# A third layer's activation queue: the first half of the exponentials ahead of the norm, the copy of the transposed norms behind the second half

## The reference

```
x = x + self_attention(norm(x))                # causal, queries = keys = values = norm(x)
x = x + cross_attention(norm(x), ctx, bias)    # a bias of 16 x 128 x 128 for each sequence
h = norm(x)
z = norm1(h) ; o = softmax(q k^T / sqrt(8)) v  # q, k, v = z @ wq + bq, z @ wk + bk, z @ wv + bv
y = h + (o @ wo + bo)
hn2 = norm2(y)
expert = argmax(hn2 @ gate_w + gate_b)         # one of 8
x = x + y + relu(hn2 @ w1[expert] + b1) @ w2[expert] + b2
```

## Time and profile before

| what | value |
|---|---|
| median of three runs | 399.95 us (399.87 to 401.6) |
| the profiled execution | 401.7 us, of which its span 400.0 us |
| mean granted TensorE clock | 0.935 |
| PE busy | 307.4 us (77% of the span) |
| DVE busy | 263.2 us (66%) |
| POOL busy | 253.2 us (63%) |
| ACT busy | 195.0 us (49%) |
| third layer | some 205 to 320 us of the span |

### The profile page before, as it was taken

One profiled execution on the slowest core, in us unless ns is written; L12 is line 12 of the kernel. 1 busy time (PEld: TensorE's weight loads), 2 busy tenths in 40 slices (PEclk: granted clock), 3 DMA queues, 4 the chain that ended last, 5 costly groups with the idle time before them and its releaser, 6 DMA issues.

```text
span 400.0 us, 10159 instructions
## 1 busy us (share of the span) xinstructions
PE 307.4 (77%) x3458; PEld 204.3 (51%) x3458; DVE 263.2 (66%) x670; ACT 195.0 (49%) x387; POOL 253.2 (63%) x361
## 2 busy tenths in 40 slices
PE   0578868767888999999688887778887751399993
PEld 0134434324766666666464444444444441399993
DVE  5137783487899899998365545476676466177873
ACT  3258775533546455655335536544545610145551
POOL 5873653346699889899996665586743554025544
PEclk9989998997899999999999989999999975599998
DMA  6109999500477887832113998433000111244110
GB/s 172 13 2 261 341 337 338 152 13 2 134 197 182 195 213 159 215 46 26 15 15 48 282 340 256 168 137 124 28 27 1 53 46 43 86 134 142 44 30 4
DMA packets 69186, 50.19 MB, mean 125 GB/s; under 512 B 36093, under 2 KB 50816, under 8 KB 69136
## 3 DMA queue, kind: packets, MB, share of 16 engines
q1 hardware_dynamic: 54960, 21.18, 22.4%
q10 hardware_dynamic: 12672, 25.20, 20.2%
q0 software_dynamic: 1504, 3.16, 2.3%
HBM read 28.48 MB, written 21.50 MB: 125 GB/s over the span
## 4 chain that ended last, share of the span: by engine, by line
PE 46%; DVE 18%; issue 14%; POOL 10%; ACT 8%; DMA 1%; SPq 0%; ACTq 0%; POOLq 0%; DVEq 0%
PE pair_banks L626 26%; PE work_bank L626 8%; DVE biased L1172 5%; PE pair_banks L629 5%; ACT xn L957 4%; DVE pair_banks L1194 3%; PE small_bank L629 3%; PE work_bank L629 3%; POOL biased L452 2%; DVE rowmax L1187 2%; DVE att L1219 2%; PE small_bank L626 1%; DVE rowsum_inv L1213 1%; POOL rstd L406 1%; ACT outT L1003 1%
## 5 line engine op out<-in xcount | busy, mean ns | idle before, releaser
L997 ACT ACTIVATE probs<-pair_banks 128x1024 f32<-128x1024 f32 x96 | 98.0, 1024 | 61.3 <-PE pair_banks L629 36.8
L452 POOL TENSOR_TENSOR biased<-biased,rowmax 128x1024 f32<-128x1024 f32 x32 | 60.5, 1897 | 16.5 <-DVE rowmax L1179 16.3
L626 PE MATMUL work_bank<-probs,vaug 128*32 128x128 f32 x1536 | 54.2, 284 | 2.7 <-DVE vaug L1157 1.2
L626 PEld LDWEIGHTS work_bank<-probs,vaug 128*32 128x32 f32 x1536 | 40.8, 113 | 17.7 <-issue 8.1
L1187 DVE TENSOR_REDUCE rowmax<-pair_banks 128x8 f32<-128x1024 f32 x32 | 38.9, 1217 | 14.0 <-PE pair_banks L626 13.9
L1172 DVE TENSOR_TENSOR biased<-pair_banks,bias_in 128x1024 f32<-128x1024 f32 x32 | 38.8, 1214 | 8.6 <-PE pair_banks L626 5.1
L519 POOL DMA_INDIRECT out<-biased x23 | 22.5, 978 | 33.4 <-DVE biased L1324 32.7
L626 PE MATMUL pair_banks<-k_lane,qT 32*128 32x512 f32 x256 | 38.6, 673 | 3.8 <-DVE biased L1172 2.4
L626 PE MATMUL pair_banks<-q_lane,kT 32*128 32x512 f32 x256 | 38.8, 678 | 1.8 <-DVE biased L1172 1.7
L629 PEld LDWEIGHTS pair_banks<-ident,biased 128*128 128x128 f32 x256 | 29.7, 149 | 18.7 <-issue 13.6
L1179 DVE TENSOR_REDUCE rowmax<-biased 128x8 f32<-128x1024 f32 x32 | 38.9, 1214 | 0.5
(11 more groups left out here) (190 smaller groups left out, 563.0 us busy)
## 6 DMA issues: line engine op xcount, KB each, us to landing
routed_rows<-cleared SPq DMA_DIRECT2D x8, 1028.0 KB, 15.2
routed_rows<-cleared ACTq DMA_DIRECT2D x8, 1028.0 KB, 6.7
bias_in<-in_w SPq DMA_DIRECT2D x16, 256.0 KB, 8.0
biased<-routed_rows SPq DMA_DIRECT2D x23, 128.5 KB, 2.1
ctx_in<-in_ctx SPq DMA_DIRECT2D x8, 128.0 KB, 6.1
att_scratch<-att SPq DMA_DIRECT2D x16, 64.0 KB, 5.4
att_rows<-att_scratch SPq DMA_DIRECT2D x16, 64.0 KB, 4.5
x_sb<-in_x SPq DMA_DIRECT2D x1, 640.0 KB, 5.4
```

Of the source, the lines that this page charges most:

```text
L452: nc.gpsimd.tensor_tensor(v, v, rowmax[:, b % 2, 8 * half:8 * half + 8].unsqueeze(2).to_broadcast([128, 8, S]), ALU.subtract).then_inc(s_s ...
L626: return nc.tensor.matmul(o, lhsT, rhs, start=start, stop=stop, **kw)
L997: nc.scalar.activation(probs[:, b % 2, 2 * half:2 * half + 2, :], pair("exp", b, half), ACT.Exp, scale=1.0 if layer(b) == CROSS else SCALE ...
```

## The change

In ACT's loop the calls of a slot change places, in the third layer alone. The first half of the exponentials runs directly behind `take_attT`, ahead of `normalise` and `last_normalise`. `take_hT` of the third layer and the early `take_hn2T` (slots 43, 45 and 47) run behind the second half of the exponentials. `take_qk` keeps its place between the two halves, the first two layers keep their order, and no other engine's code changes.

```
                 if c is not None:
                     take_attT(c)
+                if FIRST_FFN <= b < NB:
+                    exponentials(b, 0)
                 if FIRST_FFN <= b and b % 2 == 0 and q + 3 < NP:
                     normalise(q + 3)
                 if b in NORMS:
                     last_normalise(NORMS[b])
-                if FIRST_FFN <= b < NB:
-                    exponentials(b, 0)
                 if b % 2 == 1 and CROSS_PAIR <= q + 3 < NP:
                     take_qk(q + 3)
-                if b % 2 == 0 and CROSS_PAIR <= q + 3 < NP:
+                if b < FIRST_FFN and b % 2 == 0 and CROSS_PAIR <= q + 3 < NP:
+                    take_hT(q + 3)
+                if FIRST_FFN <= b < NB:
+                    exponentials(b, 1)
+                if FIRST_FFN <= b and b % 2 == 0 and CROSS_PAIR <= q + 3 < NP:
                     take_hT(q + 3)
                 if b in EARLY_HN2:
                     take_hn2T(NORMS[b])
-                if FIRST_FFN <= b < NB:
-                    exponentials(b, 1)
```

## The result

The changed kernel took 416.54 us (median of four runs, 415.73 to 421.45), beside 400.07 us for the kernel before (399.87 to 401.6): a ratio of 1.0386, 95% interval 1.032 to 1.0452, some 16 us slower. The profiled execution took 415.73 us, its span 414.0, at a mean granted clock of 0.916 where it was 0.935. It is the fastest of its four runs, and the profiled one of the kernel before the slowest of its four, so the two profiles lie 14.0 us apart where the medians lie 16.5.

A forecast was written before the change was run, and what follows sets the result against it. Time was taken to go in hand-overs between engines, with PE waiting for ACT's norms in the third layer. 8.5 us of stalls plus 6.6 of clock falls made 15.1, forecasting a median of 415.0 us, range 407.5 to 423.

The forecast's parts named there:

- The norm late by 1.08 in eight slots: Third layer, slots 32 to 40 even, 43, 45, 47: norm or last norm 1.08 us later behind exponential 0.
- 8.5 us of stalls: Third layer, PE's added waiting: 5.4 us in even slots, 0.5 in slots 37, 39, 41, 2.6 in 43, 45, 47.
- 5 x 1.08: Slots 32, 34, 36, 38, 40: late norms cost 5.4 us; behind it come 1.08 each for slots 43 and 47.
- hT and hn2T behind exponential 1 cost nothing: Third layer: copies of transposed norms, hT 1.08 us later, the delay the transposes already have, so no added cost.
- Six falls at 1.1: TensorE's clock falls behind six of the eight stalls, 1.1 us each, 6.6 us in all.
- No fall by the rule of the Trainium skill: Rival: the eight gaps are too short to lower TensorE's clock, stalls alone, 408.5 us; chance 0.15.
- Not slower: Rival: PE waits for the exponentials, exponential 1 ends 0.27 us earlier in eight slots, 397.8 us; chance 0.05.
- the change does nothing: Rival: the norm isn't due within its slot and what follows has room; nothing or a small part, chance 0.02.
- The clock stays low: Rival: after a fall TensorE's clock isn't restored before the next stall, twice the price, 426 us; chance 0.12.

The follow-up runs named there:

- e3: The whole change plus seven matmuls of constants on PE in each of the eight stalls ("filled" in the table): 406.51 us, 1.012 times the kernel before.
- e2: Kernel before with only the copies hT and early hn2T moved behind exponential 1, norms still ahead of exponential 0: 407.71 us, ratio 1.0113.
- e4: Kernel before with the third layer's norms and last norms moved ahead of the attention copy: 394.88 us, ratio 0.9759.
- e1: Kernel before with only exponential 0 moved ahead of the norms, copies hT and hn2T still ahead of exponential 1: 415.48 us, ratio 1.0292.
- e9: e4 with hT also ahead of exponential 0 in slots 38 and 40: 393.24 us, 0.9802 times the kernel before.
- e5: The change in slots 32, 34, 36 and 43 alone, other slots as in the kernel before: 407.01 us, ratio 1.0121.

## Why the prediction was right

The forecast was 415.0 us in a range of 407.5 to 423; measured were 416.54 and 416.51. Direction, place and both mechanisms (late norms, and a clock that falls behind some of the stalls) were right. The sizes of the terms were less good than their sum: one was too large, another came out by luck, and of the 16.5 us between the medians the traces place 12.7 in the interval. That the sum came within 2 us is luck in part.

- *The norm late by 1.08 in eight slots.* Right: 1.97 in place of 0.89 (2.04 in slot 47), eight times. From the exponential's start to the next one's it was 0.92 in the changed kernel, where the row had 0.90. By the Trainium skill (ScalarE: Activation LUTs, "What ACT_TABLE_LOAD costs") it was an estimated 0.95; the trace lies between the two.
- *8.5 us of stalls.* Mis-sized; e3 gives 7.0: its interval is 6.0 longer than before, and the fall that the kernel before has in slot 36 and e3 has not was worth 1.0 (8.06 against 7.08, the length of slots 32 and 34 at full clock). The term that was too large is "5 x 1.08" and one of the 1.08 behind it: slots 32, 34, 36 and 43, which have no gate behind a norm's transposes, lost 0.73 each (7.81 against 7.08). There PE had an issue gap between the output projection and the score maxes; slot 36 before:

```profile
242.21 0.39 PE L626 MATMUL small_bank<-w_fo,attT 128*128 128x128 f32 x2
242.83 1.14 PE L626 MATMUL pair_banks<-k_lane,qT 32*128 32x512 f32 x8 [0.23 <-issue]
```

  From start to start that is 0.62; behind the longer stall the gap is gone, and it is 0.39 (245.99 to 246.38). Why the gap goes is not shown. The gated slots lost the whole 1.07, the kT slots 0.17, and slots 45 and 47 with the tail 1.4, as worked out.
- *hT and hn2T behind exponential 1 cost nothing.* Right within the whole change, as slots 38 and 40 show in e3 (1.07 and 1.08). By themselves they cost 0.9 in each of the two slots, and hn2T some 0.7 in slot 47 (e2).
- *Six falls at 1.1.* The product was right by luck, since there were four falls at some 1.6. Of the 12.70 us of the interval 7.0 are stalls, so the clock took 5.7 net, and 6.7 gross, since the 1.0 of slot 36 was saved, which the forecast had left out. By slots (changed against filled in the table) the fall behind slot 40 cost 1.0, much as the price from slot 36; that behind slot 38 cost 2.4, as the low level lasted about twice as long there (262 to 269 us); and those of slots 45 and 47 cost 2.9 together, tail included (from the head of slot 45 to the tile loop 49.14 against 46.21). The remaining 0.3 lies in slots without a fall. So a price of 1.1 holds for a fall like that of slot 36, and what was missed is that the clock can stay low for longer.
- *No fall by the rule of the Trainium skill* (TensorE: Matmul & The Clock Gate, "HAM oscillation — how this bites in real kernels"). By it the time would have been 408.5; the trace shows four falls behind stalls of 1.97 to 2.04 us, so the measurement decides. e3, which takes the falls away, measured 1.012 times the kernel before, where 408.5 would be 1.021.
- *Rivals.* "Not slower" and "the change does nothing" fell with the result, and e4 shows why: there the first exponential follows the attention copy as in the change, and what makes the kernel faster is that PE's waits for norms are gone. "The clock stays low" came true in slots 38 to 39; from slot 47 on it is low in the kernel before as well, some 7 us shorter.

## What to carry to other kernels

Before an engine's queue is reordered, look at which of its results another engine already waits for, and put those first; here ACT idled 1.6 to 2.1 us ahead of most attention copies, and the norm fitted in there for a gain of 1.4 to 2.4%, while one exponential ahead of it cost 2.9% (e1), and 3.9% with the copies moved as well. A stall on TensorE can be priced twice: once in time, once in the clock behind it, which over the eight stalls here was about as much again; matmuls of constants in the stall gave back 6.7 us of the interval without making anything earlier.

## What the runs showed of the hardware that was not expected

- An issue gap on PE ahead of the score maxes was 0.36 us where PE didn't stand for the norm (e4, slot 34), 0.23 behind a wait of 0.89 and gone behind one of 1.97; in slot 38 it came back, at 0.25, when the gate's wait was shortened from 0.77 to 0.43 (e9). So 0.3 of a stall of 1.08, and 0.25 of a gain of 0.34, did not show. What the gap is, no run shows.
- The same gaps were followed by a fall of the clock in one execution and not in another: 0.89 and 0.64 in slots 38 and 40 (e5 against the kernel before), 1.97 in slot 32 (e1 and e5 against the change). Whether the change in other slots moved the falls to 38 and 40 is not shown: the mean clock of the kernel before alone went from 0.927 to 0.948 between runs.
